# The residual added in DRAM by an accumulating DMA, and the output bias added by VectorE

## What is computed

```python
def _gn(v, G=32, eps=1e-5):                       # group norm, no scale or shift
    g = v.reshape(B_, H_, W_, G, C_ // G)
    m = jnp.mean(g, axis=(1, 2, 4), keepdims=True)
    s = jnp.var(g, axis=(1, 2, 4), keepdims=True)
    return ((g - m) / jnp.sqrt(s + eps)).reshape(v.shape)

def _L0_conv_ref(inputs, Wq, bq, Wk, bk, Wv, bv, Wo, bo):
    x = inputs.reshape(B, H * W, c)
    q, k, v = x @ Wq + bq, x @ Wk + bk, x @ Wv + bv
    attn = jax.nn.softmax(jnp.einsum('bnc,bmc->bnm', q, k) * scale, axis=-1)
    return (jnp.einsum('bnm,bmc->bnc', attn, v) @ Wo + bo).reshape(B, H, W, c)

out = x + _L0_conv_ref(_gn(x), Wq, bq, Wk, bk, Wv, bv, Wo, bo)
```

## Time and profile before

| | us |
|---|---|
| median of 3 runs | 1893.12 |
| the runs | 1893.11 to 1894.78 |
| span of the profiled execution | 1891.1 |
| TensorE busy in it | 1845.2 (98%) |
| VectorE busy | 1772.4 (94%) |
| ScalarE busy | 981.6 (52%) |
| GpSimd busy | 241.8 (13%) |
| moved by DMA | 101.92 MB, 54 GB/s |

### The profile page before, as it was taken

The page is one execution under the profiler, slowest core; times in us unless marked ns, Lnnn a source line. Parts: engine busy times, 40 slices in busy tenths (PEclk is TensorE's granted clock), DMA queues, the critical chain, the costliest instruction groups (busy, mean ns, idle before and its releaser), DMA issues.

```text
span 1891.1 us, 33029 instructions
## 1 busy us (share of the span) xinstructions
PE 1845.2 (98%) x11690; PEld 1663.6 (88%) x11690; DVE 1772.4 (94%) x2793; ACT 981.6 (52%) x1347; POOL 241.8 (13%) x109
## 2 busy tenths in 40 slices
PE   8899999999999999999999999999999999999998
PEld 7789898898988888988989889889889898898987
DVE  5999999999999999999999999999999999999996
ACT  3554545646546455455465464554554654645544
POOL 1101111101111011111110110111101101101110
PEclk9999999999999999999999999999999999999999
DMA  2111211202212112121021120221211211202201
GB/s 89 45 39 51 67 48 63 67 22 67 67 44 67 29 60 67 44 67 62 27 67 66 45 67 23 66 67 44 67 51 38 67 57 54 67 22 67 67 23 45
DMA packets 29296, 101.92 MB, mean 54 GB/s; under 512 B 3681, under 2 KB 4706, under 8 KB 29282
## 3 DMA queue, kind: packets, MB, share of 16 engines
q1 hardware_dynamic: 29282, 101.73, 16.6%
HBM read 68.16 MB, written 33.55 MB: 54 GB/s over the span
## 4 chain that ended last, share of the span: by engine, by line
issue 84%; PE 6%; POOL 6%; DVE 3%; ACT 0%; POOLq 0%; DMA 0%; DVEq 0%; SPq 0%
POOL x_res L274 4%; PE ps_s L604 3%; POOL rstd L279 2%; PE ps_o L690 1%; PE ps_o L692 1%; PE ps_o L691 1%; PE ps_o L604 1%; DVE s_buf L476 1%; DVE p_lo L484 0%; DVE top L446 0%; DMA s_buf<-in_L_conv_bq_dram 0%; ACT p_hi L325 0%; DVE query_max L463 0%; ACT s_buf L331 0%; DVE g_lo L426 0%
## 5 line engine op out<-in xcount | busy, mean ns | idle before, releaser
L690 PE MATMUL ps_o<-v_hi,p_hi 128*128 128x258 f32 x2048 | 580.5, 283 | 3.2 <-DVE p_lo L484 3.2
L692 PE MATMUL ps_o<-v_hi,p_lo 128*128 128x258 f32 x2048 | 581.9, 284 | 0.0
L691 PE MATMUL ps_o<-v_lo,p_hi 128*128 128x256 f32 x2048 | 578.0, 282 | 0.0
L325 ACT ACTIVATE p_hi<-s_buf 128x1024 fp32r<-128x1024 f32 x256 | 272.5, 1065 | 554.9 <-DVE s_buf L476 554.9
L484 DVE TENSOR_TENSOR p_lo<-s_buf,p_hi 128x1024 fp32r<-128x1024 f32 x256 | 438.1, 1750 | 1.3 <-ACT s_buf L331 1.3
L604 PE MATMUL ps_s<-g_hi,h_hi 128*128 128x512 f32 x1024 | 409.1, 400 | 7.5 <-ACT s_buf L317 7.5
L317 ACT ACTIVATE s_buf<-ps_s 128x512 f32<-128x512 f32 x512 | 293.7, 608 | 214.4 <-PE ps_s L604 211.7
L604 PE MATMUL ps_s<-g_hi,h_lo 128*128 128x512 f32 x1024 | 400.6, 391 | 0.0
L604 PE MATMUL ps_s<-g_lo,h_hi 128*128 128x512 f32 x1024 | 399.7, 390 | 0.0
L690 PEld LDWEIGHTS ps_o<-v_hi,p_hi 128*128 128x128 f32 x2048 | 387.4, 189 | 6.1 <-issue 2.2
L691 PEld LDWEIGHTS ps_o<-v_lo,p_hi 128*128 128x128 f32 x2048 | 389.6, 190 | 2.8
(11 more groups left out here) (86 smaller groups left out, 2209.0 us busy)
## 6 DMA issues: line engine op xcount, KB each, us to landing
x_t<-in_x_turned_dram SPq DMA_DIRECT2D x64, 512.0 KB, 6.2
x_res<-in_x_dram SPq DMA_DIRECT2D x64, 512.0 KB, 4.7
out_dram<-o_buf SPq DMA_DIRECT2D x64, 512.0 KB, 5.3
s_buf<-in_L_conv_Wq_dram SPq DMA_DIRECT2D x1, 256.0 KB, 2.8
s_buf<-in_L_conv_Wk_dram SPq DMA_DIRECT2D x1, 256.0 KB, 2.9
s_buf<-in_L_conv_Wv_dram SPq DMA_DIRECT2D x1, 256.0 KB
s_buf<-in_L_conv_Wo_dram SPq DMA_DIRECT2D x1, 256.0 KB
s_buf<-in_L_conv_bq_dram SPq DMA_DIRECT2D x1, 1.0 KB, 3.9
```

Of the source, the lines that this page charges most:

```text
L325: nc.scalar.activation(p_hi[c][:, rows, :], s_buf[c][:, rows, :], ACT.Exp, scale=SCALE).then_inc(p_hi_done, 1)
L690: nc.tensor.matmul(ps[:, 0:VC], p_hi[c][:, m, cols], v_hi[:, m, :], start=m == 0, stop=False)
L691: nc.tensor.matmul(ps[:, 0:C], p_hi[c][:, m, cols], v_lo[:, m, :], start=False, stop=False)
L692: last = nc.tensor.matmul(ps[:, 0:VC], p_lo[c][:, m, cols], v_hi[:, m, :], start=False, stop=m == T - 1)
```

## The change

x is no longer loaded into SBUF for the residual. SP copies x from DRAM straight to the output in DRAM, half an image at a time (`residual`, in SP's block), and may do so an image ahead. VectorE's `finish` adds `out_bias` where it added `x_res`. GpSimd's addition is gone; in its place GpSimd issues the store, as a DMA that adds `o_buf` to what lies in the output (`accum_op`), after the copy of that half has landed and its four tiles are finished. SP waits at the end for copies and stores.

```diff
-            def load_rows(b, c):
-                sp.dma_start(x_res[:, c * TQ:(c + 1) * TQ, :],
-                             x_v[b, :, c * TQ:(c + 1) * TQ, :]).then_inc(x_landed[c], 16)
-
-            def rows_final(b, c):
-                after(sp, o_out, b * 8 + (4 * c + 4))
-
-            def store(b, c):
-                sp.dma_start(out_v[b, :, c * TQ:(c + 1) * TQ, :], o_buf[c][:]).then_inc(stored[c], 16)
+            def residual(b, c):
+
+                after(sp, x_copied[c], b * 16)
+                sp.dma_start(out_v[b, :, c * TQ:(c + 1) * TQ, :],
+                             x_v[b, :, c * TQ:(c + 1) * TQ, :]).then_inc(x_copied[c], 16)
...
             def body(b, first, last):
                 if not last:
                     load_turned(b + 1)
-                if not first:
-                    rows_final(b - 1, 1)
-                load_rows(b, 1)
-                if not first:
-                    store(b - 1, 1)
-                rows_final(b, 0)
-                if not last:
-                    load_rows(b + 1, 0)
-                store(b, 0)
+                    residual(b + 1, 0)
+                    residual(b + 1, 1)
...
-            def residual(b, c):
-                after(pool, x_landed[c], b * 16 + 16)
-                rows = x_res[:, c * TQ:(c + 1) * TQ, :]
-                pool.tensor_tensor(rows, rows, out_bias[:].unsqueeze(1).broadcast_to([P, TQ, C]),
-                                   ALU.add).then_inc(xres_ready, 1)
+            def store(b, c):
+
+                after(pool, x_copied[c], b * 16 + 16)
+                after(pool, o_out, b * 8 + (4 * c + 4))
+                pool.dma_start(out_v[b, :, c * TQ:(c + 1) * TQ, :], o_buf[c][:],
+                               accum_op=ALU.add).then_inc(stored[c], 16)
...
             inverse_std(0)
-            pool.wait_ge(fold_done, 4)
-            residual(0, 0)
 
             def body(b, first, last):
-                residual(b, 1)
+                if not first:
+                    store(b - 1, 1)
                 if not last:
                     inverse_std(b + 1)
-                    residual(b + 1, 0)
+                store(b, 0)
 
             images(pool, body)
+            store(B - 1, 1)
...
                 if j == 0:
-                    dve.wait_ge(xres_ready, b * 2 + (c + 1))
+                    dve.wait_ge(fold_done, 4)
                     after(dve, stored[c], b * 16)
                 dve.wait_ge(rden_done, b * 8 + (4 * c + j + 1))
                 nc.vector.scalar_tensor_tensor(out=o_buf[c][:, j, :], in0=ps_o[j][:, 0:C], scalar=rden[:, t:t + 1],
-                                               in1=x_res[:, t, :], op0=ALU.mult, op1=ALU.add).then_inc(o_out, 1)
+                                               in1=out_bias[:], op0=ALU.mult, op1=ALU.add).then_inc(o_out, 1)
```

More of the change, by code:

```diff
@@ L95, in attention_kernel @@
         out_bias = sb("out_bias", [P, C])
-        x_res = sb("x_res", [P, T, C])
         x_t = sb("x_t", [P, K, N])
@@ L145, in attention_kernel @@
         fold_done = sem("fold_done")
-        x_landed = [sem(f"x_landed{c}") for c in range(CH)]
+        x_copied = [sem(f"x_copied{c}") for c in range(CH)]
         xt_landed = [sem(f"xt_landed{k}") for k in range(K)]
-        xres_ready = sem("xres_ready")
         bn_done = sem("bn_done")
@@ L230, in _ @@
             sp.dma_start(bo_row, bo.rearrange("(a n) -> a n", a=1)).then_inc(wvo_in, 16)
-            load_rows(0, 0)
+            residual(0, 0)
+            residual(0, 1)
             def body(b, first, last):
@@ L235, in body @@
                     load_turned(b + 1)
-                if not first:
-                    rows_final(b - 1, 1)
-                load_rows(b, 1)
-                if not first:
-                    store(b - 1, 1)
-                rows_final(b, 0)
-                if not last:
-                    load_rows(b + 1, 0)
-                store(b, 0)
+                    residual(b + 1, 0)
+                    residual(b + 1, 1)
             images(sp, body)
-            rows_final(B - 1, 1)
-            store(B - 1, 1)
+            after(sp, x_copied[0], 16 * B)
+            after(sp, x_copied[1], 16 * B)
             after(sp, stored[0], 16 * B)
```

## The result

The changed kernel takes 1862.59 us in the median of 4 runs (1861.23 to 1862.75), the kernel before 1893.11 beside it. The ratio is 0.9835, with a 95% interval of 0.9824 to 0.9847. So it is faster by 1.65%. Predicted were 1864.2 us (a ratio of 0.985) and a range of 1856 to 1884.

A forecast was written before the change was run, and what follows sets the result against it. VectorE sets the pace, felt by TensorE waiting for `spread`. Profiled 1891.1 - 32.4 (wait gone) + 3.5 (last store) = 1862.2 us, plus 2.0 from span to median: 1864.2 us, ratio 0.985; range 1856 to 1884.

The forecast's parts named there:

- The wait for `spread` goes in full: TensorE's variance product waits for VectorE's `spread`, delayed by a stretched p_lo; without GpSimd's additions 1.08 x 30 images = -32.4 us.
- Nothing else is late: Behind `spread`, maximum, variance, rstd and normalisation move up 1.3 us, so h_lo and g_lo come no later for TensorE.
- the 4.3 allowed: Possible extra gain at an image's second g_lo, 0.14 x 31 = 4.3 us, in the range but not the sum.
- the term of the margins: TensorE's score tiles at an image's start have margins of 0.14 us (second g_lo) and 0.74 us (fourth).
- Bias on VectorE, copies by SP, stores in the loop: In the loop, same-size bias operations, DRAM copies and GpSimd's accumulating stores were each claimed to cost nothing.
- The end, +3.5 us: Last store in the open: 1.1 us on GpSimd for SP's 0.33 and twice the lone transfer, 0.8 + 2.7 us.
- The estimate set apart in the prediction: Last store by a fit of about 2.0 us + bytes / 436e3: 3.2 us, sum some 3 us lower.
- Rival A: GpSimd's DMA issuing for the first half's store stretches VectorE's two-input operations before the fourth g_lo: 1908 us, chance 0.09.
- D - 0.74: Cost per image of a stretch D before the fourth g_lo, margin 0.74 us; at D = 2.2, 43.8 us.
- B: The p_lo stretch belongs to the x_res transfer landing then, not to GpSimd's addition: no change, 1896.6 us, chance 0.05.
- C: Accumulating store takes over 46 us for 512 KB, so VectorE waits for the buffer; each us over costs 32; chance 0.02.

## Why the prediction was right, step by step

- **The wait for `spread` goes in full, -32.4 us.** Right in mechanism and size: 1.44 us became 0.36, so 1.08 an image. The addition alone taken out, everything else kept, gave 0.9799.
- **Nothing else is late.** Right. The margin foreseen for `spread` was 1.3 us and is 1.4. The loop gained 37.8 and not 32.4 us, and the prediction had named where the rest was without putting it into the sum: TensorE was held at the first score tile of an image, where it had only 0.14 us. Its products there, before (the earlier trace rows has the one at 949.73) and after:

```profile
949.38 0.39 PE L604 MATMUL ps_s<-h_hi,a_lo 128*128 128x512 f32 x1
...
950.06 0.40 PE L604 MATMUL ps_s<-g_lo,h_hi 128*128 128x512 f32 x1
...
932.74 0.40 PE L593 MATMUL ps_s<-h_hi,a_lo 128*128 128x512 f32 x1
...
932.98 0.39 PE L593 MATMUL ps_s<-g_hi,h_hi 128*128 128x512 f32 x1
933.21 0.40 PE L593 MATMUL ps_s<-g_lo,h_hi 128*128 128x512 f32 x1
```

  The first score product started 0.35 us after the product ahead of it and the next another 0.33; now it is 0.24 and 0.23. Set side by side over all 30 periods, the starts of the 364 products of an image differ at two places only: by 1.06 us around the variance and by 0.19 here. So 5.6 us came back at this place, more than the 4.3 allowed, because a late product also costs some 0.1 us at the one behind it. The step is the term of the margins: a margin of a tenth of a microsecond is a wait that is already there.
- **Bias on VectorE, copies by SP, stores in the loop: nothing.** Right. The o_buf rows take 484 ns as before, the wait for GpSimd's rstd stays at 0.6 us, and the stores land in a median of 5.4 us (5.3 before). The profile counts 67.1 MB written to HBM where 33.6 were, and 68.2 MB read in both, so the read that the prediction added for the accumulation isn't in that count.
- **The end, +3.5 us.** Right in sign, too small: +5.5. GpSimd took 0.86 us to issue, not 1.1, but began 0.55 us after the row. Twice the lone transfer was about right for the transfer itself: from the end of the issue to the landing are 4.3 us, where they were 2.3. What the term lacked is the time behind the landing, which it put at next to nothing: 2.9 us instead of 0.45, nearly all of it GpSimd's DRAIN. The estimate set apart in the prediction, 3.2 us from the Trainium skill's fit on the page "DMA: Bandwidth & Descriptors", section "Anatomy of one DMA — SWDGE (gpsimd) path", is under the 5.2 us that this store took from issue to landing; the measurement decides.
- **Rival A.** It fell: 128 GpSimd DMAs in two kernels, with 0.87 us of issuing each, and no p_lo over 1228 ns. What the prediction drew there from the Trainium skill (the page meant is "SBUF — State Buffer", section "Who interferes with whom"), that descriptor making doesn't meet a two-input tensor_tensor, agrees: in each of these kernels a p_lo ran beside 63 of the 64 issues, and none was stretched. The price by its formula was near: where a real addition was put at that place, D - 0.74 gave 0.82 us an image for 0.91. But D was 1.6 there and not 2.2, so even an addition would have cost 29 us and not 44, no change instead of a loss.
- **Rivals B and C.** B fell with the addition alone; C with a landing time of 5.4 us against 46.

The sum came within 1.6 us of the median partly because terms cancelled: 5.4 us more gain in the loop against 2.0 more at the end and 2.0 at the start, where nothing had been foreseen and the later rise of the clock took them. That part was luck.

## What to carry to other kernels

Look for VectorE operations whose longest duration is well over their median, and at what GpSimd runs at that moment: an addition of two SBUF tiles there costs VectorE what is left of the addition when the operation starts, and its price is the part of that for which the next consumer in line has no reserve. Name that consumer by walking VectorE's queue behind the stretched operation; the nearest margin decides, not the one that bound before, and the same stretch cost 29 us in one place and nothing in another. An accumulating DMA is a cheap way to be rid of such an addition, but put it where it has time to land: on the way in, not as the last thing that the kernel does. When you read an end, look for the landing of the last transfer as well as for its issue: here a third of the end lay behind the landing.

## What the runs showed of the hardware

- GpSimd's two-input addition of 128x1024 holds up a VectorE operation with two inputs from SBUF until it is done (such an operation of 1.22 us ends 1.08 to 1.09 us after it, in 62 cases before). In 31 additions a p_lo that started 0.15 to 0.59 us into them ran at its full 1.22 us, and the addition took 3.62 to 4.07 us instead of 2.58 to 3.14. A v_lo subtraction with one input from PSUM, 0.43 us into an addition, kept its 0.68 us.
- A one-input operation of 3.73 us lengthens VectorE's two-input ones from 1.22 to 1.30 or 1.74 us only; a memset of 2.68 us doesn't at all.
- A DMA of 512 KB issued by GpSimd holds it for 0.87 us, whether it accumulates into DRAM or into SBUF, and no VectorE operation beside it grew.
- The last accumulating store of 512 KB lands 5.2 to 5.4 us after its issue began, 128 KB after 3.0; SP's plain store of 512 KB after 2.6. GpSimd's DRAIN ends 2.7 us behind the landing of its last DMA, into DRAM and into SBUF alike. From the landing of the last store to the end of the span are 2.9 us with GpSimd's store and 0.45 with SP's.
- A wait costs TensorE more than the idle time shown: 0.8 us idle for 1.08 lost at `spread`, and 0.62 idle for 949.08 - 948.08 - 0.23 = 0.77 lost at g_lo, with 0.1 more at the product behind it.
- A product of the weight folding (128x256, float32) takes 634 ns where the granted clock is 0.50 and 379 ns where it is 1.00. A stretch ahead of the trace's first clock record is given as 1.00 though its products take 634 ns.
